# A mixture-of-experts layer whose first products swap the stationary and the moving operand: tokens in the TensorE array, weights moving in 512 columns

## The reference

```python
    x = x + _L0_xattn_ref(_layernorm(x, axis=-1), ctx_1024, ...)
    x = x + _L0_attn_ref(_layernorm(x, axis=-1), ...)
    x = x + _L0_ffn_ref(_layernorm(x, axis=-1), ...)
...
        gate_logits = jnp.einsum('bpd,de->bpe', x, W_gate)
        top_w, top_idx = jax.lax.top_k(gate_logits, K)          # K = 2 of E = 8
        top_w = jax.nn.softmax(top_w, axis=-1)
...
        for e in range(E):
            h = jax.nn.gelu(jnp.einsum('bpd,dm->bpm', x, W_in[e]) + b_in[e], approximate=False)
            y = jnp.einsum('bpm,md->bpd', h, W_out[e]) + b_out[e]
            out = out + combine[..., e, None] * y
```

## Time and profile before

| what | value |
|---|---|
| median of 3 runs | 1342.96 us (1339.91 to 1345.90) |
| span of the profiled execution | 2069.7 us |
| mean granted TensorE clock in the profiled execution | 0.548 |
| PE busy in the span | 2018.5 us |
| DVE busy in the span | 956.7 us |
| ACT busy in the span | 814.5 us |

### The profile page before, as it was taken

One profiled execution on the slowest core, in us unless ns is written; L12 is line 12 of the kernel. 1 busy time (PEld: TensorE's weight loads), 2 busy tenths in 40 slices (PEclk: granted clock), 3 DMA queues, 4 the chain that ended last, 5 costly groups with the idle time before them and its releaser, 6 DMA issues. The chain is left out here.

```text
span 2069.7 us, 22326 instructions
## 1 busy us (share of the span) xinstructions
PE 2018.5 (98%) x9274; PEld 1067.0 (52%) x9274; DVE 956.7 (46%) x787; ACT 814.5 (39%) x950; POOL 123.7 (6%) x118
## 2 busy tenths in 40 slices
PE   7999999999999999999999999998799999999998
PEld 4444444444444444444444444424577777878776
DVE  4345545454555454545554545564443244334332
ACT  2444444444444444444444444441133233323321
POOL 0000000000000000000000000000020000000010
PEclk6555555555555555555555555555555555555555
DMA  5200000000000000000000000014034524443430
GB/s 196 49 21 1 21 1 21 21 1 21 21 1 21 1 21 21 1 21 21 1 21 1 21 1 1 2 71 164 21 130 129 173 89 134 128 159 103 134 113 9
DMA packets 56378, 107.90 MB, mean 52 GB/s; under 512 B 5874, under 2 KB 6002, under 8 KB 56272
## 3 DMA queue, kind: packets, MB, share of 16 engines
q1 hardware_dynamic: 53568, 101.55, 14.4%
q0 software_dynamic: 2720, 5.09, 1.2%
HBM read 95.57 MB, written 12.14 MB: 52 GB/s over the span
## 5 line engine op out<-in xcount | busy, mean ns | idle before, releaser
L498 DVE TENSOR_TENSOR p_sum<-p_sum,as_p 128x2048 f32<-128x2048 f32 x252 | 577.7, 2292 | 556.3 <-ACT as_p L465 556.0
L465 ACT ACTIVATE as_p<-as_s 128x1024 f32<-128x1024 f32 x512 | 496.6, 1022 | 368.2 <-PE as_s L394 365.1
L409 PE MATMUL as_o<-as_p,as_v 128*32 128x512 f32 x2048 | 414.6, 950 | 0.0
L394 PEld LDWEIGHTS as_s<-as_q_hi,as_k_hi 32*128 32x128 f32 x1024 | 49.0, 181 | 274.0 <-issue 274.0
L409 PEld LDWEIGHTS as_o<-as_p,as_v 128*32 128x32 f32 x2048 | 69.5, 132 | 225.1 <-issue 221.7
L1135 ACT ACTIVATE se_h<-se_hp,se_b_cur 128x160 f32<-128x160 f32 x128 | 43.5, 391 | 288.3 <-PE se_hp L1050 288.3
L394 PE MATMUL as_s<-as_q_lo,as_k_hi 32*128 32x512 f32 x1024 | 144.5, 558 | 0.0
L394 PE MATMUL as_s<-as_q_hi,as_k_lo 32*128 32x512 f32 x1024 | 144.5, 557 | 0.0
L346 POOL TENSOR_TENSOR as_c_lo<-as_c,as_c_hi 128x512 fp32r<-128x512 f32 x60 | 76.5, 1275 | 1111.7 <-ACT as_c_hi L457 1111.7
L1050 PEld LDWEIGHTS se_hp<-se_xg_hi,se_wi_hi 128*128 128x128 f32 x512 | 116.0, 311 | 47.4 <-issue 45.8
L394 PE MATMUL as_s<-as_q_hi,as_k_hi 32*128 32x512 f32 x1024 | 134.6, 517 | 2.4 <-ACT as_p L465 1.6
(11 more groups left out here) (238 smaller groups left out, 1932.5 us busy)
## 6 DMA issues: line engine op xcount, KB each, us to landing
ei_wi<-w_in SPq DMA_DIRECT2D x32, 1024.0 KB, 7.2
ei_wo<-w_out SPq DMA_DIRECT2D x32, 1024.0 KB, 5.4
as_c<-ctx_t SPq DMA_DIRECT2D x16, 1024.0 KB, 5.3
slots_scratch<-as_zeros SPq DMA_DIRECT2D x10, 256.0 KB, 3.8
acc_scratch<-as_zeros SPq DMA_DIRECT2D x10, 256.0 KB, 3.9
pq_w<-xw_in SPq DMA_DIRECT2D x1, 2048.0 KB, 11.8
se_tokens<-slots_scratch SPq DMA_DIRECT2D x7, 256.0 KB, 5.4
x_sb<-x SPq DMA_DIRECT2D x4, 256.0 KB, 3.6
```

The costliest lines, as they stand in the source:

```text
L394: last = nc.tensor.matmul(s[r][:, j % 2 * NQ:(j % 2 + 1) * NQ], keys[rows, g, t * P:(t + 1) * P], queries[rows, g, :], start=(part == 0), ...
L409: last = nc.tensor.matmul(o[j * D:(j + 1) * D, :], v[b][:, t, feats], p[step % PR][:, j * NQ:(j + 1) * NQ], start=(t == 0), stop=(t == KT ...
L465: nc.scalar.activation(p[step % PR][:, pair * 2 * NQ:(pair + 1) * 2 * NQ], s[r][:, :], ACT.Exp, scale=SCALE).then_inc(p_ready[step % PR], 1)
L498: nc.vector.tensor_tensor(sums, sums, p[step % PR][:, :], ALU.add).then_inc(p_summed[step % PR], 1)
```

## The change

`hidden` is turned round. The main 128 tokens become the stationary operand and the chunk's 512 columns of W_in move: 12 f32r matmuls of 512 columns. The 32 tail tokens are taken in plain f32 (`xt`) against the unsplit weights `wi[mc]`, as 16 matmuls of 128 columns in four 32-column tiles of the array. Both land with tokens on partitions, in one PSUM buffer `hp`. Since the second layer and the bias need hidden units on partitions, DVE copies the result to SBUF (`pre`, `tail_pre`, in `keep_hidden`), and PE transposes it, four blocks for the main tokens and one for the tail (`turn_hidden`), into the PSUM tile `ht`, from where ACT applies Gelu in four instructions of 128x128 and four of 128x32.

The order is changed with it. PE's last output of an expert moves behind the first hidden of the next; `turn_hidden(e, mc)` stands behind the output of the chunk before. ACT's and DVE's split of W_out moves ahead of the Gelu and of the split of `h`. The load of the next expert's W_in waits for `h_done` in place of `wi_lo_ready`.

```diff
-    hp = [ctx.enter_context(nc.psum_tensor(f"se_hp{b}", [P, MT, 2 * P], F32)) for b in range(2)]
+    pre, tail_pre = sb("pre", [P, MC]), sb("tail_pre", [P, P])
+    xt = sb("xt", [P, ET, D])
+    hp = ctx.enter_context(nc.psum_tensor("se_hp", [P, 2, MC], F32))
+    ht = ctx.enter_context(nc.psum_tensor("se_ht", [P, 2, MC], F32))
...
-                        sp.wait_ge(wi_lo_ready, n + 1)
+                        sp.wait_ge(h_done, 2 * (n + 1))
                         inputs.load_in(sp, w_in, e + 1, mc)
...
-                wait_reuse(pe, h_ready, MT * (n - 1))
+                    pe.wait_ge(xt_ready, e + 1)
+                for a, (lhs, rhs) in enumerate(((xg_hi, wi_hi), (xg_hi, wi_lo), (xg_lo, wi_hi))):
+                    for d in range(ET):
+                        last = nc.tensor.matmul(hp[:, 0, :], lhs[:, d, 0:P], rhs[b][:, d, :],
+                                                start=(a == 0 and d == 0), stop=(a == 2 and d == ET - 1))
+                last.then_inc(h_done, 1)
+                for d in range(ET):
+                    for j in range(MT):
+                        last = nc.tensor.matmul(hp[j * D:(j + 1) * D, 1, 0:P], xt[:, d, :], wi[mc][:, d, j * P:(j + 1) * P],
+                                                start=(d == 0), stop=(d == ET - 1))
+                last.then_inc(h_done, 1)
+
+            def turn_hidden(e, mc):
+                n = NMC * e + mc
+                wait_reuse(pe, h_ready, 2 * MT * n)
+                pe.wait_ge(pre_ready, 2 * n + 1)
                 for t in range(MT):
-                    for a, (lhs, rhs) in enumerate(((wi_hi, xg_hi), (wi_lo, xg_hi), (wi_hi, xg_lo))):
-                        for d in range(ET):
-                            last = nc.tensor.matmul(hp[b][:, t, 0:CAP], lhs[b][:, d, t * P:(t + 1) * P], rhs[:, d, :],
-                                                    start=(a == 0 and d == 0), stop=(a == 2 and d == ET - 1))
-                    if t % 2 == 1:
-                        last.then_inc(h_done, 1)
+                    last = nc.tensor.transpose(ht[:, 0, t * P:(t + 1) * P], pre[:, t * P:(t + 1) * P], ident[:, :])
+                last.then_inc(h_turned, 1)
+                pe.wait_ge(pre_ready, 2 * n + 2)
+                nc.tensor.transpose(ht[:, 1, 0:P], tail_pre[:, :], ident[:, :]).then_inc(h_turned, 1)
...
             def expert(e, last):
...
+                    output(e - 1, NMC - 1)
+                turn_hidden(e, 0)
+                hidden(e, 1)
+                if not first:
                     join_parts(e - 1)
-                hidden(e, 1)
                 output(e, 0)
+                turn_hidden(e, 1)
...
+                    split_out(e, mc)
+                    if mc == 0:
+                        act.wait_ge(b_ready, e + 1)
+                    act.wait_ge(h_turned, 2 * n + 1)
                     for t in range(MT):
-                        act.wait_ge(h_done, 2 * n + t // 2 + 1)
-                        nc.scalar.activation(h[b][:, t, :], hp[b][:, t, 0:CAP], ACT.Gelu,
+                        nc.scalar.activation(h[b][:, t, 0:P], ht[:, 0, t * P:(t + 1) * P], ACT.Gelu,
...
+                    act.wait_ge(h_turned, 2 * n + 2)
+                    for t in range(MT):
+                        nc.scalar.activation(h[b][:, t, P:CAP], ht[:, 1, t * D:(t + 1) * D], ACT.Gelu,
...
+            def keep_hidden(n):
+                dve.wait_ge(h_done, 2 * n + 1)
+                wait_reuse(dve, h_turned, 2 * n)
+                nc.vector.tensor_copy(pre[:, :], hp[:, 0, :]).then_inc(pre_ready, 1)
+                dve.wait_ge(h_done, 2 * n + 2)
+                nc.vector.tensor_copy(tail_pre[:, :], hp[:, 1, 0:P]).then_inc(pre_ready, 1)
```

More of the change, by code:

```diff
@@ L942, in send_to_experts @@
     h_done, h_ready, h_hi_ready, h_lo_ready, y_done = map(sem, ("h_done", "h_ready", "h_hi_ready", "h_lo_ready", "y_done"))
+    pre_ready, h_turned, xt_ready = map(sem, ("pre_ready", "h_turned", "xt_ready"))
     y_ready, parts_ready, joined, tail_y_ready, tail_done = map(sem, ("y_ready", "parts_ready", "joined", "tail_y_ready", "tail_done"))
@@ L1016, in gather @@
                 pe.wait_ge(sel_ready, QT)
-                for x, bank, done in ((r.x_hi, turn, hi_gathered), (r.x_lo, hp[0], lo_gathered)):
+                for x, bank, done in ((r.x_hi, turn, hi_gathered), (r.x_lo, lo_bank, lo_gathered)):
                     for d in range(ET):
@@ L1062, in output @@
                     wait_reuse(pe, y_ready, e)
-                    wait_reuse(pe, tail_y_ready, e)
                 if mc == NMC - 1 and ends:
-                    tail_output(mc, b).then_inc(tail_done, 1)
+                    tail_output(e, mc, b).then_inc(tail_done, 1)
                     main_output(mc, b).then_inc(y_done, 1)
@@ L1069, in output @@
                     main_output(mc, b)
-                    tail_output(mc, b).then_inc(y_done, 1)
+                    tail_output(e, mc, b).then_inc(y_done, 1)
             def main_output(mc, b):
@@ L1078, in main_output, with tail_output @@
                 return last
-            def tail_output(mc, b):
+            def tail_output(e, mc, b):
+                pe.wait_ge(h_ready, 2 * MT * (NMC * e + mc + 1))
+                if mc == 0:
+                    wait_reuse(pe, tail_y_ready, e)
                 for m in range(MT):
@@ L1091, in expert @@
             def expert(e, last):
+                first = isinstance(e, int) and e == 0
                 hidden(e, 0)
-                if isinstance(e, int) and e == 0:
+                if first:
                     output_biases()
@@ L1105, in expert @@
                 output(e, 2)
-                output(e, 3, last)
+                turn_hidden(e, 3)
             gather()
             rolled(pe, NX, expert)
+            output(NX - 1, NMC - 1, True)
         @block.scalar
@@ L1129, in expert @@
                         split_in(e + (mc + 1) // NMC, (mc + 1) % NMC)
+                    if mc == NMC - 1 and not last:
+                        act.wait_ge(turned, e + 1)
+                        nc.scalar.activation(xt[:, :, :], turn[:, :, P:CAP], ACT.Copy).then_inc(xt_ready, 1)
+                        nc.scalar.activation(xg_hi[:, :, :], turn[:, :, 0:CAP], ACT.Copy).then_inc(xg_hi_ready, 1)
                     wait_reuse(act, y_done, n - 1)
-                    if last and mc == NMC - 1:
-                        split_out(e, mc)
+                    split_out(e, mc)
+                    if mc == 0:
+                        act.wait_ge(b_ready, e + 1)
+                    act.wait_ge(h_turned, 2 * n + 1)
                     for t in range(MT):
-                        act.wait_ge(h_done, 2 * n + t // 2 + 1)
-                        nc.scalar.activation(h[b][:, t, :], hp[b][:, t, 0:CAP], ACT.Gelu,
+                        nc.scalar.activation(h[b][:, t, 0:P], ht[:, 0, t * P:(t + 1) * P], ACT.Gelu,
                                              bias=b_cur[:, mc * MT + t:mc * MT + t + 1]).then_inc(h_ready, 1)
[L1137 to L1141, removed]
+                    act.wait_ge(h_turned, 2 * n + 2)
+                    for t in range(MT):
+                        nc.scalar.activation(h[b][:, t, P:CAP], ht[:, 1, t * D:(t + 1) * D], ACT.Gelu,
+                                             bias=b_cur[:, mc * MT + t:mc * MT + t + 1]).then_inc(h_ready, 1)
             split_in(0, 0)
@@ L1176, in split_out, with keep_rows, keep_tail @@
                                         ALU.subtract).then_inc(wo_lo_ready, 1)
-            def keep_parts(e):
+            def keep_rows(e, index):
+                dve.wait_ge(y_done, NMC * index)
                 wait_reuse(dve, joined, e)
                 nc.vector.tensor_copy(parts[:, :], tp[:, :]).then_inc(parts_ready, 1)
-            def keep_tail(e):
-                dve.wait_ge(joined, e + 1)
-                dve.wait_ge(meta_loaded, 32 * (e + 1))
+                dve.wait_ge(meta_loaded, 32 * index)
                 wait_reuse(dve, landed, 32 * e)
-                nc.vector.tensor_scalar(tail_y[:, :], tp[0:D, :], tail_meta[:, bass.ds(e + 1, 1)], None, ALU.mult).then_inc(tail_y_ready, 1)
+                nc.vector.tensor_scalar(y[:, :], yp[:, :], meta[:, bass.ds(index, 1)], None, ALU.mult).then_inc(y_ready, 1)
+            def keep_tail(e, index):
+                dve.wait_ge(joined, index)
+                dve.wait_ge(meta_loaded, 32 * index)
+                wait_reuse(dve, landed, 32 * e)
+                nc.vector.tensor_scalar(tail_y[:, :], tp[0:D, :], tail_meta[:, bass.ds(index, 1)], None, ALU.mult).then_inc(tail_y_ready, 1)
+            def keep_hidden(n):
[4 more added lines that the diff above has]
+                nc.vector.tensor_copy(tail_pre[:, :], hp[:, 1, 0:P]).then_inc(pre_ready, 1)
             def expert(e, last):
-                wait_reuse(dve, h_ready, NMC * MT * e)
+                first = isinstance(e, int) and e == 0
+                wait_reuse(dve, h_ready, 2 * NMC * MT * e)
```

(36 more changed lines are left out.)

4 lines of the change are left out of this document (2 added, 2 removed).

## The result

The changed kernel takes 1310.28 us (median of 4 runs, 1308.91 to 1311.37), the one before 1343.65 in the same runs: a ratio of 0.976 (95% interval 0.974 to 0.978), 33 us less. The forecast was 1218 with a range from 1165 to 1300. The direction was right, and the size nearly four times too large.

The account below looks back on a forecast made before the run. PE was taken as the bound, busy 2018.5 of 2069.7 us. The experts' 450 us would become 325 (268 of PE work, DVE nearly equal, a fifth for hand-overs, the bare end), saving 125 from 1343: 1218 us, range 1165 to 1300.

Parts of the forecast that it names:

- From this execution to the timed runs: Step converting the profiled 2069.7 us to the timed 1342.96: the experts before taken as 450 us, falling to 325.
- The second inference: In the experts, about half the work runs at 2.4 GHz and half at 1.2, from 301 us at full clock against 450.
- PE's sum: Per chunk of hidden at the lower clock: 5.2 + 1.7 + 1.2 = 8.1 us against 10.3, 2.2 saved.
- PE's 33 us over the experts: PE's work in the experts at 2.4 GHz falls from 301 to 268 us.
- The tail side by side: Hidden's sixteen tail matmuls run as four tiles at once: 1.65 us, 1.7 with the entry, at the lower clock.
- the rival by which it is slower: Tail matmuls in hidden run one after the other, 6.6 us in place of 1.65: 1412 us; chance 0.05.
- the bare end: After the last expert's output 2, chunk 3's Gelu, split and hand-overs lie uncovered, about 4 us once.
- The cover: Output n-1 hides DVE's copies (1 us a chunk); hidden n+1 hides Gelu and split (about 5 us).
- DVE as the next bound: In the experts, DVE at 30.4 us plus gaps nearly equals PE's 33.5; as rival, 1228 to 1263, chance 0.13.
- The 0.4 us eight times an expert: On DVE, each `h_lo` waits for its `h_hi`, bringing 30.4 us an expert to 33.6.
- My fifth on top for hand-overs: A fifth added to the experts because PE and DVE, equally full, don't overlap wholly: 322 us.
- The clock does not recover: Rival: transposes and waits break PE's stream every chunk, half the experts' work stays at 1.2 GHz: 1299 us; chance 0.12.

Follow-up runs that it names:

- the second profile of the kernel before: The kernel before, unchanged, profiled again to have its profile at the clock of the timed runs: 1342.55 us, at a clock of 0.964.

## Why the prediction was wrong, and where it was right

- **The step that failed** is "From this execution to the timed runs". It took the experts as what is left of 1343 us when the other stages are subtracted, and each of those was scaled down too far: attention "at least 724", measured 853; the 93 us behind it "about 59", measured 71; the first 80 "between 44 and 80", measured 67. Together 845 (with 62 for the first) were subtracted where 990 stood. That left 480 to 516, and 410 to 445 with a tenth for hand-overs in attention, from which I took 450; measured were 350.
- Why they scale less. PE's own matmuls in attention shrink less than the clock rises, each kind of them. One round of them takes 10.37 us in the first profile (699.64 to 710.01, clock 0.56) and 6.66 in the second (599.96 to 606.62, clock 1.00), where the clock alone would give 5.8: twelve projections 4.70 and 2.99, the scores 2.51 and 1.81, the weighted sum 3.16 and 1.86. The long ones start 0.234 us apart at 1.00 (as in the changed hidden, 0.93 for four), not 512 columns at 2.4 GHz, 0.213; what holds them back no run shows. The Trainium skill, "TensorE: Matmul & The Clock Gate", section "Back-to-back issue gap", gives 512/2.4 + 2.5, or 216 ns, as the gap of an isolated matmul, and 131 ns as the measured pace of a stream; the long matmuls here start at least 224 ns apart, above both. In a stream of weight loads and matmuls both set the spacing, the same section of the Trainium skill says, so that the 0.213 us of 160 columns, which the prediction held against it, do not contradict it.
- **The second inference fell with it**: that half of the experts' work runs at 1.2 GHz in the timed runs. In the second profile of the kernel before the clock is low only up to about 1030 us: it stays at 0.50 through the first two hidden, rises in the long matmuls of output 0, and is 1.00 in every later hidden, of the same matmuls. So there was no clock to win back but in the opening, where the changed kernel has 0.72 against 0.54 and is 10.3 us ahead: by an estimate from these rows (32.66 x 0.54 against 22.32 x 0.72) 1.6 by less work and the rest, close to 9 us, by its clock. That the same 48 matmuls went with 0.50 in one profile and 1.00 in the other is shown; why is not settled.
- **PE's sum was right for a chunk**: 2.2 us at the lower level, so 1.1 at 2.4 GHz; measured were 5.58 against 4.00 + 0.52, 1.06. In part this is luck. Both sides came out about a tenth above half of what was put down (5.58 and 4.52, against 5.16 and 4.05), which cancels; the tail output's row, for one, was read as one at the lower level and had 0.56.
- That PE's 33 us over the experts (301 to 268 in the text) meet the 33.1 of the stage is luck as well. By the rows above, PE's busy time times its clock fell from 338.74 x 0.94 to 301.58 x 0.96, some 29 us; about 8 came from the clock of the opening, and 4 were lost to an idle PE (11.9 us, then 15.9). This is an estimate from rounded clocks. Halved and taken from 1343, the sum would have said 1310. What made the forecast 125 was all put on top, by the clock.
- **The tail side by side** was right: 1.02 us, not four times that, and the rival by which it is slower fell. So were the five transposes (0.6 expected at 2.4 GHz, 0.52 found) and the bare end (2.3 us found of some 4).
- **The cover** was right. The copies under it were put at 1 us a chunk, 32 in all; without it 57 us are lost, more than the whole gain, in part by the clock.
- **DVE as the next bound** was half right. It is busy 29.54 us of 36.49 in a middle expert (30.4 forecast), but a further 0.69 us a chunk costs 2 to 3 us in all: PE bounds, and DVE shows at the experts' borders, where moving one instruction to ACT gave 6 us. The 0.4 us eight times an expert that each `h_lo` was to wait is in no row: the earlier trace rows have 7.5 us idle ahead of all 64, and the profile after 6.7. My fifth on top for hand-overs hid a PE slower than I took it, by 0.02 us for each long matmul; the 325 came out close to 317.5 for a partly wrong reason.
- "The clock does not recover", at 1299, came nearest among the rivals, but not by its mechanism: the clock was 1.00 in the experts from 1014 us to their last outputs.

## What to carry to other kernels

A profile taken at another clock than the timed runs gives the work, not the remainder: scale the saving itself, and do not get a small stage by subtracting large ones that were scaled by rule, since their whole error lands on it. Two profiles are compared between the same instructions, not the same microseconds. Where each matmul brings weights of its own and moves few columns (128 and 160 here), count matmuls and not columns; turning the operands round can then pay for transposes and copies, if other PE work stands between the matmuls and the transposes that wait for the copy. When PE is the bound and DVE is nearly as full, look at the borders of the loop first: one instruction moved to ACT, which is busy for 22.69 of 36.49 us, was worth 6 us, where reordering PE gave some 4, not clear of the noise.

## What the runs showed of the hardware that was not expected

- 128 and 160 moving columns cost the same, 0.113 us a matmul at 2.4 GHz and (for 160) 0.213 at 1.2, when each loads 128 columns of f32r weights.
- Sixteen f32 matmuls of 128 columns in four column tiles take 1.02 us at 2.4 GHz, little more than four of 512 columns (0.99): the same columns in all, and four times the instructions cost almost nothing.
- The first profile of the kernel before has a granted clock of 0.55 all through attention, between the two levels; in the nine profiles after it the clock there is 1.00. The same instructions took 1316 us in the one and 853 in the other, 0.65 where the clocks stand as 0.55.
- In the second profile of the kernel before, PE is busy from 1000 to 1028 us with hidden's short matmuls and the biases, and the clock stays at 0.50; it rises within the long matmuls that follow, and the same short ones then keep 1.00.
